# A graph layer and a Mamba block on one core: five pairs of units get their product with C in one GpSimd operation each

## What is computed

```python
delta = softplus(einsum('blr,dr->bld', dt, W_dt) + b_dt)
A = -exp(A_log)                           # 1024 channels x 16 states
def step(h, ins):
    d_t, B_t, C_t, u_t = ins
    dA = exp(d_t[..., None] * A)
    h = dA * h + (d_t * u_t)[..., None] * B_t[:, None, :]
    y_t = einsum('bds,bs->bd', h, C_t)
    return h, y_t
...
y = y + u * Dp
y = y * silu(z)
```

## Time and profile before

| | us |
|---|---|
| median of three runs | 3736.74 |
| the three runs | 3736.74, 3719.45, 3741.27 |
| the profiled execution's own time | 3739.78 |
| its span | 3738.0 |

### The profile page before, as it was taken

The page is one execution under the profiler, slowest core; times in us unless marked ns, Lnnn a source line. Parts: engine busy times, 40 slices in busy tenths (PEclk is TensorE's granted clock), DMA queues, the critical chain, the costliest instruction groups (busy, mean ns, idle before and its releaser), DMA issues.

```text
span 3738.0 us, 43683 instructions
## 1 busy us (share of the span) xinstructions
PE 3471.2 (93%) x11130; PEld 1965.5 (53%) x11130; DVE 3521.1 (94%) x2877; ACT 2962.9 (79%) x6578; POOL 3411.8 (91%) x1703
## 2 busy tenths in 40 slices
PE   5899999999999999999999999999999999999887
PEld 3555555555555555555555555555555555555433
DVE  0499999999999999999999999999999999999998
ACT  2588788888878888888888788788878888887874
POOL 0399999999999999999999999999999999999998
PEclk9899999999999999999999999999999999999999
DMA  3111101111100111110111110111110111110110
GB/s 112 53 56 59 59 12 49 56 58 58 58 22 40 56 58 58 58 47 15 58 55 58 59 55 12 53 56 58 58 58 9 53 55 58 58 54 9 46 51 9
DMA packets 50720, 183.68 MB, mean 49 GB/s; under 512 B 7356, under 2 KB 33220, under 8 KB 42086
## 3 DMA queue, kind: packets, MB, share of 16 engines
q1 hardware_dynamic: 48898, 174.17, 12.1%
q10 hardware_dynamic: 1636, 7.83, 0.5%
HBM read 164.15 MB, written 17.83 MB: 49 GB/s over the span
## 4 chain that ended last, share of the span: by engine, by line
POOL 44%; issue 26%; PE 14%; ACT 8%; DVE 7%; POOLq 1%; DMA 0%; ACTq 0%; DVEq 0%; SPq 0%
POOL st L425 30%; POOL st L416 8%; PE y_ps L773 5%; DVE st L967 4%; ACT dec L491 3%; POOL delta L398 3%; POOL du_sb L406 2%; DVE st L955 2%; PE d_ps L810 2%; PE d_ps L830 1%; PE g L926 1%; POOL rstd L383 1%; PE d_ps L852 1%; ACT L491 1%; DVE u L992 1%
## 5 line engine op out<-in xcount | busy, mean ns | idle before, releaser
L425 POOL TENSOR_TENSOR st<-st,bc 128x1024 f32<-128x1024 f32 x1024 | 2404.9, 2364 | 162.3 <-DVE st L967 161.9
L967 DVE TENSOR_TENSOR_SCAN st<-dec,st 128x1024 f32<-128x1024 f32 x1024 | 2316.3, 2279 | 11.7 <-ACT dec L491 5.1
L773 PE MATMUL y_ps<-st,ident 128*128 128x512 f32 x4096 | 1928.1, 605 | 130.1 <-POOL st L425 129.0
L491 ACT ACTIVATE dec<-delta,decay 128x254 f32<-128x254 f32 x4096 | 1691.7, 464 | 309.7 <-DVE st L967 307.5
L773 PEld LDWEIGHTS y_ps<-st,ident 128*128 128x128 f32 x4096 | 751.1, 192 | 957.4 <-issue 654.3
L955 DVE TENSOR_TENSOR st<-du,bc 128x1024 f32<-128x1024 f32 x736 | 886.4, 1204 | 2.2 <-ACT du L477 2.2
L416 POOL TENSOR_TENSOR st<-du_sb,bc 128x1024 f32<-128x1024 f32 x288 | 680.7, 2364 | 0.1
L539 ACT ACTIVATE u<-d_ps,bconv,chan 128x256 f32<-128x256 f32 x256 | 129.8, 557 | 258.7 <-PE d_ps L810 258.6
L810 PE MATMUL d_ps<-xnT,wxz 128*128 128x256 f32 x1024 | 261.9, 401 | 70.0 <-DVE u L992 69.3
L992 DVE SCALAR_TENSOR_TENSOR u<-d_ps,chan,u 128x250 f32<-128x250 f32 (+2 forms) x768 | 307.1, 474 | 6.1 <-ACT u L539 6.1
L810 PEld LDWEIGHTS d_ps<-xnT,wxz 128*128 128x128 f32 x1024 | 197.3, 198 | 143.6 <-DVE u L992 103.6
(11 more groups left out here) (111 smaller groups left out, 2534.3 us busy)
## 6 DMA issues: line engine op xcount, KB each, us to landing
bc<-bc_dram SPq DMA_DIRECT2D x64, 2048.0 KB, 9.8
xg<-x_dram SPq DMA_DIRECT2D x32, 256.0 KB, 11.5
x_dram<-xg SPq DMA_DIRECT2D x32, 256.0 KB, 2.0
last_x<-x_dram SPq DMA_DIRECT2D x32, 256.0 KB, 2.6
out_dram<-last_x SPq DMA_DIRECT2D x32, 256.0 KB, 2.1
bc<-w_inT_dram ACTq DMA_DIRECT2D x1, 4096.0 KB, 13.9
adjt<-adjT_dram SPq DMA_DIRECT2D x32, 128.0 KB, 11.2
bc<-w_out_dram ACTq DMA_DIRECT2D x1, 2048.0 KB
```

The lines of the kernel that those rows point to most:

```text
L425: nc.gpsimd.tensor_tensor(st[:, sl, :, :, :], st[:, sl, :, :, :], bc[:, p, 1, SU * q:SU * q + SU, None, :].to_broadcast([P, SU, 2, T]), AL ...
L491: a = nc.scalar.activation(dec[:, v % 2, s, j, :].rearrange("p (b t) -> p b t", b=PAIR)[:, :, 1:], delta[:, p, 2 * i + j, :].rearrange("p ...
L773: mm = nc.tensor.matmul(y_all, ident[:, :], st[:, sl, s, :, :].rearrange("p j t -> p (j t)"), start=False, stop=(q == Q - 1 and s == SU - ...
L967: nc.vector.tensor_tensor_scan(h, dec[:, v % 2, :, :, :].rearrange("p s j t -> p (s j t)"), h, 0.0, ALU.mult, ALU.add).then_inc(S["scanned ...
```

## The change

For the pairs of units that begin with 2, 4, 8, 16 and 24 POOL no longer multiplies the first unit at its own v. At the v of the second unit one operation covers both slots (which lie side by side) with 2048 elements per partition, waits for both scans, and adds 2 to `c_times`. All else that POOL did at v stays at its v. PE, DVE, ACT and SP are unchanged.

```diff
+C_PAIRS = (2, 4, 8, 16, 24)
...
                     if scan:
-                        c_product(pool, k, p, v)
+                        if v - 1 in C_PAIRS:
+                            c_product(pool, k, p, v - 1, 2)
+                        elif v not in C_PAIRS:
+                            c_product(pool, k, p, v, 1)
...
-            def c_product(pool, k, p, v):
+            def c_product(pool, k, p, v, n):
                 if v == 0:
                     wait(pool, "c_loaded", 16 * k + 16)
-                wait(pool, "scanned", U * k + v + 1)
+                wait(pool, "scanned", U * k + v + n)
                 q, sl = v % Q, v % SLOTS
-                nc.gpsimd.tensor_tensor(st[:, sl, :, :, :], st[:, sl, :, :, :],
-                                        bc[:, p, 1, SU * q:SU * q + SU, None, :].to_broadcast([P, SU, 2, T]),
-                                        ALU.mult).then_inc(S["c_times"], 1)
+                units = st[:, sl:sl + n, :, :, :].rearrange("p w s j t -> p (w s) j t")
+                nc.gpsimd.tensor_tensor(units, units,
+                                        bc[:, p, 1, SU * q:SU * (q + n), None, :].to_broadcast([P, SU * n, 2, T]),
+                                        ALU.mult).then_inc(S["c_times"], n)
```

## The result

The changed kernel takes 3762.61 us, the median of six runs from 3760.52 to 3766.08. Six runs of the kernel before gave a median of 3726.09, from 3719.45 to 3741.27. The ratio is 1.0086, with a 95% interval of 1.0069 to 1.0103: 0.9% slower, above the forecast range of 3708 to 3755. The profiled execution after took 3760.52 us, 20.7 more than the profiled one of before.

What follows compares the result with a forecast made beforehand. DVE was taken as the bound. Gate gain -8.7, pair (24, 25) loss +4.4 and last group -0.3 sum to -4.6 us, rounded to 5, from the 3736.74 median: 3732 us, range 3708 to 3755.

Steps and rivals of the forecast that it cites:

- DVE sets the period: Steady groups: DVE busy 109.69 of 110.4 us; POOL's savings shorten a group only through DVE's gate wait, 0.51 us.
- the pair (24, 25): Near group's end: POOL waits about 3.8 us, late sums make DVE stand 0.1 to 0.2 us; loss 4.4 us.
- The pair's price: POOL's 2048-element product: 4.47 us start to start against 4.62 for two singles, saving 0.15 us each time.
- The first pairs' gain: Pairs (2, 3) and (4, 5): gate 0.30 us earlier in 29 groups, gain 8.7 us.
- The pair (8, 9): Edge product and `deviations` run first and cover the time to scan 9's end; no gain or loss.
- the pair (4, 5): POOL is behind here, so both scans are over when it arrives and nothing is added to its queue.
- Cost nil, but the cover is thin: Pair (16, 17): PE's sums 1.0 us late, 1.3 against DVE; 0.8 of 2.07 us cover left for unit 22's decays.
- the clock falls ahead of the sum of unit 16 as well: PE's 1.9 us stand there drops its clock; 4.3 us per fall, ten falls 43 us: 3775; chance 0.11.
- A second rival: PE's clock falls less or more often at the existing place; none left gives 3700, five more 3748; chance 0.17.
- The ten old falls: PE's clock falls to 1.2 GHz for 10.3 us ahead of a u projection; DVE waits 3.2 us each.
- all three of its own signs: Wrong if DVE waits in over two places, 0.95-clock groups move by over three, or period changes over 0.4 us.

Runs made afterwards that it cites:

- e8: Kernel before with only pairs (2, 3), (4, 5), (8, 9) joined, plus PE matmuls of zeros ahead of the third u projection: 3699.34 us, ratio 0.9912.
- e6: Changed kernel plus two PE matmuls adding zero in the stand ahead of the sum of unit 16: 3719.13 us, ratio 0.9965 to before.
- e7: Kernel before plus two PE matmuls of zeros in the stand ahead of the third u projection: 3711.26 us, ratio 0.9943.
- e1: Changed kernel's code with only the pair (16, 17) joined: 3765.07 us, ratio 1.0075 to before.
- e3: Changed kernel's code with only the pair (24, 25) joined: 3722.16 us without a stray execution, ratio 0.9974 to before.

## Why the prediction was wrong

**What held.** DVE sets the period; POOL's saved time became a longer stand ahead of the pair (24, 25): 3.4 us in the three groups without a fall, 4.9 to 5.0 where the scans came late, forecast 3.8. The pair's price was right. The first pairs' gain was right by the mechanism, 0.3 us at the gate in e8. The pair (8, 9) costs nothing. But it and the pair (4, 5) do not always find both scans over, as the prediction had it: in every second group POOL stands 0.4 to 0.7 us for scan 5 and 0.4 us for scan 9. The pair (24, 25) makes DVE stand 0.1 to 0.2 us at the att product: 0.18 measured.

**The step that failed** is "Cost nil, but the cover is thin" at the pair (16, 17). It had PE's stand at 1.9 us; it was 2.2 and 2.6 by turns. POOL ran as forecast: its pair began 63.8 us after the group's first scan in every group (forecast 1902.7 - 1838.8 = 63.9), straight behind the injection of unit 20, when scan 17 had been over for 0.6 or 0.9 us. But PE was through with the `diag` matmuls 0.5 or 0.8 us sooner than before, by the gate's 0.5 us and, in every second group, 0.3 more, and the forecast had left that time where it was. It had 0.8 us of cover against the lateness of the sums, and that nearly held (e6). But it left the clock at its higher level. The rival "the clock falls ahead of the sum of unit 16 as well" is what happened, and it got a chance of 0.11. Its price was off on both sides: 4.3 us for each of ten falls was the forecast, and there were 25 of about 1.7 us each, 42 us in the groups from the second to the 29th. A fall here lasted 3.4 us; I had taken the 10.3 us of the other place for it. What should have raised its chance stood in the rows: PE fell after a stand of 2.02 us, and the change makes a second one of that length in every group.

**A term that was left out:** the turn of the loop, 0.8 to 1.1 us in every second group, 11.4 us in 13 groups. The small stand was forecast, what it uncovers was not.

**A second rival came true beside it, and that was luck.** The ten old falls are all gone, which the prediction had as a case of its own (3700 us, with no new loss). In the profiled executions this hides some 31 us of the loss. By all three of its own signs the forecast was wrong: DVE waits in more than two places, the count of groups with an old fall moved by ten, and the period went from 110.4 to 112.2 us in the mean.

**The account** of the 28 groups from the second to the 29th, against the kernel before without its falls (110.37 us per group, 3090 us): waits for decays 42 us, the turn 11 us, the att product 28 x 0.18 = 5 us, the gate -28 x 0.48 = -13 us, together +45 us. Measured are 3142 us, 51 more. The 6 us between the two are in DVE's busy time, 3527.4 us where it was 3521.1 for the same 2877 instructions: where an instruction has to wait, it no longer overlaps with the one before it, and the idle row does not count that. Taken from start to start, against the usual distance of the same two instructions in e8, the items are 45, 12.5, 5 and -14 us, with 1.6 us more in waits too short for a row: 50 of the 51. Before had nine falls in that stretch, about 31 us, which the changed kernel has not; so the two profiled executions differ by only 20.7 us.

One wording of the prediction has to be put right: the old fall stands ahead of the third u projection of a group, the one at v = 4, not the second.

## What to carry to other kernels

Joining two operations saves the fixed part once (0.15 us here from start to start) and makes the consumer of the first wait for the second (2.3 us). Before doing it, look at each consumer's stand, not only at whether what follows has cover: on PE a stand of some 2 us may cost more in clock afterwards than in waiting. Where such a stand can't be avoided, matmuls that add zero to the open sum kept the clock up and cost nothing that could be measured (e7's groups take 110.38 us, those of before without a fall 110.37). And with a total that wanders by over 20 us from one run to the next, take the period of a group without a fall to judge an edit of 0.3 us.

## What was not expected of the hardware

- The clock's fall hangs on where a stand lies in time. The same stand of 2.02 us brought one in every third group. At unit 16 all 13 stands of 2.6 us did and 12 of the 15 of 2.2 us; in e6, with 0.5 to 0.9 us there, none did. The changed kernel has no fall ahead of the third u projection, though PE stands 2.12 us there in every second group; e6, with the same stand and no falls at unit 16, has six. So falls at one place seem to take away those at the other, which no run isolates (e1 has both).
- Falls differ in length at the same 1.2 GHz level: 10.3 us ahead of the third u projection in the kernel before, 3.4 us there in six groups of e3, 3.4 us at unit 16 in the changed kernel.
- A stand of 0.18 us ahead of the loop's turn uncovered 0.8 to 1.1 us of DVE, each time that the loop turned back.
